# A four-layer convolution and state-space network: sums by accumulating DMAs, more products on GpSimd, and the image kept in memory

## The reference

```python
def selective_scan(u, delta, A, B, C, D):
    A = jnp.clip(A, -5.0, 5.0)
    dA = jnp.einsum('bld,dn->bldn', delta, A)
    dB_u = jnp.einsum('bld,bld,bln->bldn', delta, u, B)
    ...
    x = jnp.cumsum(dB_u * c, axis=1) / (c + 1e-06)
    y = jnp.einsum('bldn,bln->bld', x, C)
    return y + u * D
...
return h_out + w_out + x
```

## Time and profile before

| | |
|---|---|
| median of 3 runs | 17881.85 us (17880.17 to 17891.42) |
| span of the profiled execution | 17874.5 us |
| axis stage h, first to last weighting | 1343.9 to 8794.7 us |
| axis stage w, first to last weighting | 8897.4 to 16327.0 us |
| most tiles of an axis stage | 115.6 to 115.7 us |
| mean granted TensorE clock | 0.984 of full |

### The profile page before, as it was taken

How to read it: one execution, slowest core, us unless ns; L and a number is a source line. 1 busy time by engine, 2 the same in 40 slices (tenths; PEclk the granted TensorE clock), 3 DMA queues, 4 the chain that set the end, 5 groups by cost and what they waited for, 6 DMA issues and landing times. The chain is left out here.

```text
span 17874.5 us, 307595 instructions
## 1 busy us (share of the span) xinstructions
PE 15666.8 (88%) x66328; PEld 8928.0 (50%) x66424; DVE 16925.9 (95%) x45263; ACT 15656.0 (88%) x24641; POOL 15706.1 (88%) x10824
## 2 busy tenths in 40 slices
PE   8878898888888888888788888888888888888788
PEld 3325555555555555555455555555555555553233
DVE  7999999999999999999999999999999999997799
ACT  7769999999999999999799999999999999995588
POOL 4669999999999999999799999999999999996577
PEclk9999999999999999999899999999999999999899
DMA  2011011111011110111100000000000000000000
GB/s 41 16 19 11 9 11 12 12 11 11 9 12 12 11 12 10 10 12 11 13 11 12 12 9 12 12 12 12 11 10 11 12 12 11 12 11 12 21 16 14
DMA packets 785299, 227.32 MB, mean 13 GB/s; under 512 B 755377, under 2 KB 758093, under 8 KB 783437
## 3 DMA queue, kind: packets, MB, share of 16 engines
q1 hardware_dynamic: 780084, 204.64, 9.2%
q10 hardware_dynamic: 3352, 2.14, 0.1%
HBM read 143.66 MB, written 62.96 MB: 12 GB/s over the span
## 5 line engine op out<-in xcount | busy, mean ns | idle before, releaser
L1409 POOL TENSOR_TENSOR h_sm<-h_sm,h_wr 128x768 f32<-128x768 f32 x2944 | 5396.2, 1833 | 448.9 <-DVE h_wr L1134 348.7
L1409 POOL TENSOR_TENSOR w_sm<-w_sm,w_wr 128x768 f32<-128x768 f32 x2944 | 5395.3, 1833 | 369.3 <-DVE w_wr L1134 261.2
L1134 DVE SCALAR_TENSOR_TENSOR h_wr<-h_pz,h_bct,h_rbuf 128x192 f32<-128x192 f32 x11776 | 4292.3, 416 | 92.5 <-PE h_pz L1586 75.3
L1134 DVE SCALAR_TENSOR_TENSOR w_wr<-w_pz,w_bct,w_rbuf 128x192 f32<-128x192 f32 x11776 | 4292.2, 417 | 90.9 <-PE w_pz L1586 74.8
L1586 PE MATMUL h_pz<-h_xr,h_tri 128*128 128x384 f32 x6912 | 3079.1, 528 | 582.2 <-DVE h_wr L1134 469.9
L1586 PE MATMUL w_pz<-w_xr,w_tri 128*128 128x384 f32 x6912 | 3069.2, 526 | 571.8 <-DVE w_wr L1134 468.3
L1259 ACT ACTIVATE w_cbuf<-w_pe_e,w_consts 128x1024 f32<-128x1024 f32 x2304 | 2573.9, 1117 | 567.2 <-PE w_pe_e L1565 423.4
L1259 ACT ACTIVATE h_cbuf<-h_pe_e,h_consts 128x1024 f32<-128x1024 f32 x2304 | 2573.4, 1117 | 559.6 <-PE h_pe_e L1565 413.5
L1108 DVE SCALAR_TENSOR_TENSOR h_xr<-h_cbuf,h_bct,h_pdx 128x192 f32<-128x192 f32 x6912 | 2547.1, 413 | 150.5 <-ACT h_cbuf L1259 98.1
L1108 DVE SCALAR_TENSOR_TENSOR w_xr<-w_cbuf,w_bct,w_pdx 128x192 f32<-128x192 f32 x6912 | 2546.5, 413 | 133.4 <-ACT w_cbuf L1259 98.1
L1297 ACT ACTIVATE w_rbuf<-w_pe_e,w_consts 128x1024 f32<-128x1024 f32 x2304 | 2579.8, 1120 | 18.4 <-DVE w_wr L1134 16.0
(11 more groups left out here) (379 smaller groups left out, 27336.4 us busy)
## 6 DMA issues: line engine op xcount, KB each, us to landing
h_lt<-pieces_s SPq DMA_DIRECT2D x512, 96.0 KB, 4.9
w_lt<-pieces_s SPq DMA_DIRECT2D x512, 96.0 KB, 4.3
pieces_s<-h_pieces SPq DMA_DIRECT2D x384, 48.0 KB, 2.1
pieces_s<-w_pieces SPq DMA_DIRECT2D x384, 48.0 KB, 2.1
h_xt<-first_s SPq DMA_DIRECT2D x34, 128.0 KB, 6.3
w_xt<-first_s SPq DMA_DIRECT2D x34, 128.0 KB, 3.1
m_u<-hn_s SPq DMA_DIRECT2D x32, 128.8 KB, 2.7
m_u<-slots_s SPq DMA_DIRECT2D x32, 128.8 KB, 2.6
```

The lines of the kernel that those rows point to most:

```text
L1134: ins = v.scalar_tensor_tensor(dst, pz[:, P % 2, m * DX:(m + 1) * DX], bct[:, par, g * 2 * NX + NX + n + m:g * 2 * NX + NX + n + m + 1], r ...
L1409: tt(sm[:, g], sm[:, g], wr[:, u % 3], ALU.add).then_inc(s_add, 1)
```

## The change

- acc is gone from the axis stages. The image lies in memory (acc_s). In h, ScalarE writes into stage, two rings of 8 columns, and SP stores 8 columns at a time, in pieces of 32 bytes. In w, SP loads the two rows of a tile into image, GpSimd adds, SP stores them. The filter loads the whole image in three parts.
- With the room, tb has a ring of 6 and there are two new buffers of 8 x 192 for each group, held and sent. Of the 24 units of a half pass, the blocks u // 2 in SENT (0, 2, 4, 6, 8; four pairs each) are no longer added by GpSimd. The first goes into held; each of the other four goes into sent and is added onto held by a DMA that GpSimd issues (send). Two adds at u = 22 put held into sm (add_held). So GpSimd has 13 + 2 adds a half pass instead of 23.
- OTHER has 29 pairs instead of 18. scale_c is gone: all odd pairs have B in the triangles, and those of OTHER too. WIDE has 19 pairs instead of 24. triangles has three parts, the last of two pairs behind the third ratio group.
- Two biases are numbers instead of columns of consts.
- The loop of SP is unrolled for its first turn.

```diff
+        held = sb("held", [128, 2, 8, DX])
+        sent = sb("sent", [128, 2, 8, DX])
+        tb = sb("tb", [128, 6, 2, TB])
...
-        OTHER = [P for P in range(PAIRS) if P % 8 == 7 or P % 16 == 11]
-        WIDE = [P for P in range(PAIRS) if P % 8 in (1, 5)]
-        SCALED = WIDE
-        NS2, RING = len(SCALED), 3
+        OTHER = [P for P in range(4, PAIRS) if P % 8 in (3, 7) or P % 16 == 13]
+        WIDE = [P for P in range(PAIRS) if P % 2 == 1 and P not in OTHER]
+        SCALED = [P for P in range(PAIRS) if P % 2 == 1]
+        NS2, RING = len(SCALED), 6
         OWN = PAIRS - len(OTHER)
+
+        SENT = (0, 2, 4, 6, 8)
+        KEPT = [u for u in range(UN) if u // 2 not in SENT]
+        LATE = KEPT[-2]
+        ADD_NO, NA = {}, 0
+        for u in KEPT[1:]:
+            NA += 1
+            ADD_NO[u] = NA
+            if u == LATE:
+                NA += 2
+                HELD_NO = NA
+        NA += 1
+        ND = len(SENT) - 1
...
-        CUTS = (0, 1)
+        CUTS = (0, 1, 2)
...
+                def store_columns(G, made):
+                    sp.wait_ge(s_fe, made)
+                    ring = G % 2 * 8 if isinstance(G, int) else sp.snap((G & 1) * 8)
+                    cols4 = acc_s.rearrange("p (b h w) -> p b h w", b=2, w=W)
+                    sp.dma_start(cols4[:, bass.ds(val(upper(G, 3)), 1), :, bass.ds(val((G & 7) * 8), 8)].squeeze(1),
+                                 stage[:, :, bass.ds(ring, 8)]).then_inc(s_st, 16)
+
+                def load_image(T, p):
+                    if not (isinstance(T, int) and T < 2):
+                        sp.wait_ge(s_st, val(T * 16 - 16))
+                    sp.dma_start(image[:, p, :], acc_s[:, bass.ds(val(T * TB), TB)]).then_inc(s_img, 16)
+
+                def store_image(T, p):
+                    sp.wait_ge(s_res, val(T + 2))
+                    sp.dma_start(acc_s[:, bass.ds(val(T * TB), TB)], image[:, p, :]).then_inc(s_st, 16)
+
...
+                def place(g, u, at):
+
+                    if u in KEPT:
+                        i = KEPT.index(u)
+                        return sm[:, g, at, :] if i == 0 else wr[:, i % 3, at, :]
+                    k, at = SENT.index(u // 2), u % 2 * 4 + at
+                    return held[:, g, at, :] if k == 0 else sent[:, k % 2, at, :]
+
+                def room(T, g, u):
+
+                    done = T * 2 * NA + g * NA
+                    if u in KEPT:
+                        i = KEPT.index(u)
+                        if i == 0:
+                            dve.wait_ge(s_add, done)
+                        elif i > 3:
+                            dve.wait_ge(s_add, done + NA + ADD_NO[KEPT[i - 3]])
+                        else:
+                            before = max(n for n in range(1, len(KEPT)) if n % 3 == i % 3)
+                            dve.wait_ge(s_add, done + ADD_NO[KEPT[before]])
+                        return
+                    k, first = SENT.index(u // 2), isinstance(T, int) and T == 0
+                    if u % 2 == 1:
+                        return
+                    if k == 0:
+                        if not first:
+                            dve.wait_ge(s_add, done - NA + HELD_NO)
+                    elif not (first and g == 0 and k < 3):
+                        dve.wait_ge(s_da, T * 32 * ND + (g * ND + k - 2) * 16)
+
                 def weighted(T, par, P):
 
                     g, n = P // 48, (P % 48) * 2
                     ch, u = P // 8, (P % 48) // 2
                     if P % 8 == 0:
                         dve.wait_ge(s_r, T * GRP + 3 * ch + 5)
-                    if P % 2 == 0:
-                        held = {0: 0, 1: UN - 2, 2: UN - 1, 3: UN - 1}.get(u, UN + u - 3)
-                        if not (isinstance(T, int) and T == 0 and g == 0 and u == 0):
-                            dve.wait_ge(s_add, T * 2 * UN + g * UN + held)
+                    if P % 2 == 0 and not (isinstance(T, int) and T == 0 and g == 0 and u == KEPT[0]):
+                        room(T, g, u)
                     dve.wait_ge(s_z, T * PAIRS + P + 1)
                     for m in range(2):
-                        at = (P % 2) * 2 + m
-                        dst = sm[:, g, at, :] if u == 0 else wr[:, u % 3, at, :]
                         ins = v.scalar_tensor_tensor(
-                            dst, pz[:, P % 2, m * DX:(m + 1) * DX],
+                            place(g, u, (P % 2) * 2 + m), pz[:, P % 2, m * DX:(m + 1) * DX],
                             bct[:, par, g * 2 * NX + NX + n + m:g * 2 * NX + NX + n + m + 1],
                             rbuf[:, ch % 2, (n + m) % 16, :], ALU.mult, ALU.mult)
                     ins.then_inc(s_wd, 1)
...
-                def scale_c(T, q, ch, bc_done):
-
-                    for P in OTHER:
-                        if P // 8 != ch:
-                            continue
-                        g, n = P // 48, (P % 48) * 2
-                        act.wait_ge(s_c, T * GRP + 3 * ch + 3)
-                        if bc_done is not None:
-                            act.wait_ge(s_fe, bc_done)
-                        for m in range(2):
-                            c = cbuf[:, ch % 2, (n + m) % 16, :]
-                            ins = a.activation(c, c, ACT.Identity,
-                                               scale=bct[:, q, g * 2 * NX + n + m:g * 2 * NX + n + m + 1])
-                        ins.then_inc(s_cb, 1)
...
-                scale_c(0, 0, 0, 3)
+                triangles(0, 0, 0, 2, None, True)
...
-                    image = acc[:, bass.ds(1 + upper(T, 5) * (H + 1) + (T & 31) * 2, 2), 1:1 + W]
-                    tt(image, image, to3, ALU.add).then_inc(s_res, 1)
+                    pool.wait_ge(s_img, T * 16 + 16)
+                    tt(image[:, p, :], image[:, p, :], to[:], ALU.add).then_inc(s_res, 1)
 
                 def add(T, g, u):
+                    i, k = KEPT.index(u), SENT.index(u // 2 - 1) if u // 2 - 1 in SENT else 0
+                    if u % 2 == 0 and k > 1:
+                        pool.wait_ge(s_da, T * 32 * ND + (g * ND + k - 1) * 16)
                     pool.wait_ge(s_wd, T * PAIRS + g * 48 + 2 * u + 4)
-                    if u > 1:
-                        pool.wait_ge(s_add, T * 2 * UN + g * UN + UN + u - 1)
-                    tt(sm[:, g], sm[:, g], wr[:, u % 3], ALU.add).then_inc(s_add, 1)
+                    if i > 1:
+                        pool.wait_ge(s_add, T * 2 * NA + g * NA + NA + ADD_NO[u] - 1)
+                    tt(sm[:, g], sm[:, g], wr[:, i % 3], ALU.add).then_inc(s_add, 1)
+
+                def send(T, g, k):
+
+                    nc.gpsimd.dma_start(held[:, g].rearrange("p a d -> p (a d)"),
+                                        sent[:, k % 2].rearrange("p a d -> p (a d)"),
+                                        accum_op=ALU.add).then_inc(s_da, 16)
+
+                def add_held(T, g):
+
+                    pool.wait_ge(s_da, T * 32 * ND + (g + 1) * ND * 16)
+                    for n in range(2):
+                        pool.wait_ge(s_add, T * 2 * NA + g * NA + NA + HELD_NO - 2 + n)
+                        tt(sm[:, g], sm[:, g], held[:, g, 4 * n:4 * n + 4], ALU.add).then_inc(s_add, 1)
 
                 def product(T, P):
 
                     g, n, ch = P // 48, (P % 48) * 2, P // 8
                     if P == OTHER[0]:
                         pool.wait_ge(s_dxs, T + 1)
-                    pool.wait_ge(s_cb, T * len(OTHER) + OTHER.index(P) + 1)
+                    pool.wait_ge(s_c, T * GRP + 3 * ch + 3)
                     c2 = cbuf[:, ch % 2, n % 16:n % 16 + 2, :]
                     tt(c2, c2, dxs[:, g:g + 1, :].broadcast_to([128, 2, DX]), ALU.mult).then_inc(s_xo, 1)
 
                 def tree(T, g):
-                    pool.wait_ge(s_add, T * 2 * UN + g * UN + 2 * UN - 1)
+                    pool.wait_ge(s_add, T * 2 * NA + g * NA + 2 * NA - 1)
                     tt(sm[:, g, 0:2], sm[:, g, 0:2], sm[:, g, 2:4], ALU.add).then_inc(s_tr, 1)
...
-                        if u > 0:
+                        if u in KEPT[1:]:
                             add(T, g, u)
+                        if u % 2 == 0 and u // 2 - 1 in SENT[1:]:
+                            send(T, g, SENT.index(u // 2 - 1))
                         for P in OTHER:
                             if (P - 7) // 2 == U:
                                 product(T, P)
+                        if u == LATE:
+                            add_held(T, g)
                         if u == UN - 1:
                             tree(T, g)
                         if U == 10 and not first and not vertical:
-                            residual(T - 1, T * 6 + O_AT)
+                            residual(T - 1, 1 - par, T * 6 + O_AT)
                         if not last:
...
+                def load_rows(n):
+                    b2, lo, hi = CHUNKS[n]
+                    r = 1 + b2 * (H + 1)
+                    sp.dma_start(acc[:, r + lo:r + hi, 1:1 + W], image[:, b2, lo:hi, :]).then_inc(s_img[n], 16)
```

136 lines of the change are left out of this document (89 added, 47 removed).

## The result

The changed kernel takes 18947.06 us (median of 4 runs, 18944.83 to 18956.03) against 17881.01 before: a ratio of 1.0596, 95% interval 1.0581 to 1.0611. It is 6% slower. The prediction was 17,800, with a range up to 18,300.

A forecast was written before the change was run, and what follows sets the result against it. VectorE was taken to set the pace, three other engines close behind. Terms summed to -0.9 us a tile, -115 over 128 tiles; with +36 for the image, -79, giving 17,800 us, range 17,420 to 18,300.

The forecast's parts named there:

- At the middle of the tile ... no loss there: GpSimd's tail at mid-tile: prefix scan and ScalarE's 2.3 us stretch the time available to about 22 us, so no loss.
- The accumulating DMAs: nothing, if each takes under 6.7 us: GpSimd's sends of 768 KB: each expected at 4.7 us (3.2 to 7.7), costing nothing below 6.7 us.
- rival 2: Accumulating transfers too slow: at 7.7 us each, plus 6 us a tile, about 18,570 us; chance 18 in 100.
- rival 3: Third piece through memory to lt comes late for TensorE: 3 us a tile, about 18,180 us; chance 7 in 100.
- VectorE minus 6.2: VectorE's work per tile: six scaled pairs less save 3.9 us, five wide products less 2.3 us.
- TensorE plus 0.5: TensorE can't quite follow VectorE where three odd pairs in a row are GpSimd's: 0.5 us a tile, between 0 and 1.5.
- ScalarE's waits plus 1.8: VectorE's waits for ScalarE, at block 7 and the next blocks, grow from 1.5 to 3.3 us a tile.
- GpSimd plus 3.0 at the tile's end: Adds, products, send and tree ahead of next tile's product 7 take 22.0 us where 19.0 are there: 3.0 us late.
- The image plus 36: Image in memory: stores at stage ends 12 and 3 us, filter load 1, shared DMA engines 20; 36 us in all.

The follow-up runs named there:

- the steps alone: The changed kernel with GpSimd making the steps of dt at place 22, ahead of the held adds, tree and product 55: 18,718.01 us, ratio 1.0467.
- SyncE's part of it: The changed kernel with the x loads of every fourth tile issued behind the lt load and not ahead of it: 18,878.65 us, ratio 1.0560.
- small transfers: The changed kernel with each accumulating transfer cut to one of its eight blocks, issues, waits and order kept: 18,401.88 us, ratio 1.0289.
- Taking the tail away: On top of the mended order, the second half's held adds and tree moved behind the next tile's first product: 18,175.08 us, ratio 1.0167.
- the mended order: The changed kernel with dt's steps at place 22, the first half's held adds and tree behind product 55, x loaded behind lt: 18,402.65 us, ratio 1.0294.

## Why the prediction was wrong, step by step

- **"At the middle of the tile ... no loss there"** is the step that failed first. It asked whether product 55 is in time for TensorE, and forgot that the steps of dt stand behind product 55 on the same engine and that VectorE's scan waits for them. It was 5.5 us a tile of wait; 229 us came back with the steps alone, 544 with the whole order (SyncE's part of it, alone, gave 68).
- **"The accumulating DMAs: nothing, if each takes under 6.7 us"** failed too. The median was 6.0 and 5.8 us, inside the bounds of 3.2 to 7.7 and under the threshold. But the limit has to hold for each one: those that met the pieces and lt took longer (issued at 5044.5, its waiter released at 5052.2), and GpSimd waited 3.6 us a tile. Their bytes cost 545 us, counting lt. So rival 2 and rival 3 both came true in part and together, and were priced as alternatives. The Trainium skill (DMA: Bandwidth & Descriptors, Issuing engines are not separate DMA queues) says that all issuers' transfers share 16 engines; the trace agrees: lt landed in 4.3 us without them and in 6.7 with them. The prediction had this beside rival 3 only.
- **VectorE minus 6.2** was nearly right as work (busy 112.4 to 107.3, 5.1 less) and wrong as worth. This is the third step that failed. The triangles' part was 6 x (0.65 - 0.46) = 1.1 us a tile, 146 us; it measured 134. The products' part returned 0.8 of 5.1 us even without a transfer. The prediction had itself said that VectorE's saving is worth only what the other three let through, and then counted it in full, with **TensorE plus 0.5** (range to 1.5) where 3.7 was measured.
- **ScalarE's waits plus 1.8** had the wrong sign: VectorE's wait for C, 1.5 us a tile before, is not in the list of the changed kernel. The edit of the biases, which was not costed, took 6.5 us of ScalarE's work a tile and gave 58 us of time.
- **GpSimd plus 3.0 at the tile's end** was right in mechanism and too large. Its list of 22.0 us has five products, as in the first half; at the tile's end there are only four (91, 93, 95 and 7 of the next tile), so by its own prices it is 21.0 and late by 2.0. Of the 47.0 us that TensorE waited for GpSimd's products in 16 tiles, 17.5 stand at product 7, 1.1 us a tile: 1.5 to 2.2 us in each of nine tiles, little or nothing in the others. Another 23.5 stand some 8 us ahead of the dx copy, at product 91. They are the transfers' bytes: 0.5 us is left of them with small transfers and nothing with none. Taking the tail away gave 1.8 us a tile in the mended order. GpSimd's total was met (97.5 us a tile, predicted some 97). The issue, taken at 0.9, is recorded at 0.87 us but adds only 0.6 from start to start (5057.91 to 5058.52).
- **The image plus 36** measured 3 us in the kernel without transfers.
- **TensorE's clock** was in no term. The prediction priced every wait at its length; with the new stalls the mean granted clock was 0.954, against 0.984 before.

The balance that was wanted: -58 biases, -134 triangles, +3 image, +1,252 for the sums. Of the last, 772 went with orders mended (544 + 228); the other 480 stand while the transfers and the 29 products do. How these 480 divide between bytes and issues at that order is not measured. With only the middle mended, bytes cost 429 us and issues and waits 332, against the same kernel without transfers.

## What to carry to other kernels

Work that can't start before its data can't use spare time that came earlier: cost a freed engine over each stretch between two such points, everything on its list counted (here 47.5 us against 43.2), and not over the tile. For every item behind a tail that grows, list all its waiters; the next product was checked here, and the small step behind it stopped VectorE. And before an engine is relieved, run the kernel with that work left out and nothing in its place: with the order mended and the products moved, but a third of the adds missing and no transfer, it took 17,642 us, only 53 less than the kernel that makes every add. That bounds what the sums could gain in this order, even by transfers that cost nothing.
